# Pacing GpSimd's indirect transfers and thinning TensorE's waits in a graph and mixer network

## The reference, cut to what matters

```python
xn = _layernorm(x, axis=-1)
x = x + _L1_gnn_ref(xn, ...) + _L1_mix_ref(xn[None], ...)[0]
x = x + _L1_ffn_ref(_layernorm(x, axis=-1)[None], ...)[0]
```

```python
h = (x @ W.T).reshape(n, heads, out_ch)
e = jax.nn.leaky_relu(alpha_src[src] + alpha_dst[dst], NEG_SLOPE)
e = jnp.exp(e - m[dst])
alpha = e / (s[dst] + 1e-16)
out = jax.ops.segment_sum(alpha[:, :, None] * h[src], dst, num_segments=n)
```

## Time and profile before

| | |
|---|---|
| median of 3 runs | 10682.89 us (10681.89 to 10693.84) |
| span of the profiled execution | 10685.8 us |
| TensorE busy | 6666.1 us, 62% |
| VectorE busy | 5067.1 us, 47% |
| GpSimd busy | 3649.9 us, 34% |
| ScalarE busy | 2678.2 us, 25% |

### The profile page before, as it was taken

The page is one execution under the profiler, slowest core; times in us unless marked ns, Lnnn a source line. Parts: engine busy times, 40 slices in busy tenths (PEclk is TensorE's granted clock), DMA queues, the critical chain, the costliest instruction groups (busy, mean ns, idle before and its releaser), DMA issues. The chain is left out here.

```text
span 10685.8 us, 95917 instructions
## 1 busy us (share of the span) xinstructions
PE 6666.1 (62%) x27702; PEld 4202.5 (39%) x27702; DVE 5067.1 (47%) x10547; ACT 2678.2 (25%) x6047; POOL 3649.9 (34%) x3597
## 2 busy tenths in 40 slices
PE   5456656689657536649984663665664577626856
PEld 4452333334444433336753332333443233313434
DVE  6453046522477733461126544436545788733231
ACT  0012100022244404302223430331222455312211
POOL 2522346400246436602032763462111355120021
PEclk5558877799779857769996776677787799868968
DMA  3110033210246433304423333331022122210012
GB/s 94 38 34 13 4 89 91 56 46 27 69 136 179 120 98 88 91 6 131 168 83 96 95 90 78 101 91 32 15 67 61 44 68 69 68 58 7 7 60 76
DMA packets 440710, 758.91 MB, mean 71 GB/s; under 512 B 172573, under 2 KB 268795, under 8 KB 437521
## 3 DMA queue, kind: packets, MB, share of 16 engines
q0 software_dynamic: 182080, 437.26, 15.1%
q1 hardware_dynamic: 239987, 295.32, 8.8%
q10 hardware_dynamic: 18136, 20.19, 0.6%
HBM read 669.59 MB, written 82.56 MB: 70 GB/s over the span
## 5 line engine op out<-in xcount | busy, mean ns | idle before, releaser
L2448 POOL DMA_INDIRECT R<-table,edges x1248 | 1243.2, 996 | 861.0 <-issue 306.3
L2500 DVE TENSOR_TENSOR acc<-acc,PS 125x256 f32 (+3 forms) x1664 | 704.9, 424 | 1242.4 <-PE PS L2519 376.5
L2519 PE MATMUL PS<-R,hot 128*125 128x256 f32 (+1 forms) x1664 | 644.8, 476 | 418.0 <-issue 203.4
L2527 PE MATMUL PS<-iota_b,ident_b 128*128 128x500 bf16 x1728 | 764.7, 449 | 5.7 <-PEq L71 5.7
L2268 PE MATMUL PS<-S,hotT 125*128 125x100 bf16 (+1 forms) x6240 | 362.9, 218 | 575.1 <-DVE hotT L2375 460.4
L2460 ACT ACTIVATE R<-R,TW 128x128 f32<-128x128 f32 (+1 forms) x1248 | 493.4, 431 | 685.0 <-DMA R<-table,edges 644.7
L2519 PEld LDWEIGHTS PS<-R,hot 128*125 128x125 f32 x1664 | 361.6, 234 | 683.1 <-issue 520.3
L2517 PE MATMUL PS<-R,hot 128*125 128x258 f32 x1664 | 438.0, 416 | 203.6 <-DVE acc L2498 117.5
L2268 PEld LDWEIGHTS PS<-S,hotT 125*128 125x128 bf16 x6240 | 315.3, 112 | 623.8 <-DVE hotT L2375 429.7
L2448 POOL DMA_INDIRECT xx<-table,edges x416 | 412.8, 992 | 384.4 <-PE PS L2519 312.5
L2448 POOL DMA_INDIRECT room<-table,edges x416 | 425.6, 1023 | 330.2 <-PE PS L2519 191.7
(11 more groups left out here) (719 smaller groups left out, 13558.8 us busy)
## 6 DMA issues: line engine op xcount, KB each, us to landing
rowb<-slo_row SPq DMA_DIRECT2D x260, 250.0 KB
W<-in_L_ffn_W1p SPq DMA_DIRECT2D x32, 1024.0 KB
W<-in_L_ffn_W2p SPq DMA_DIRECT2D x32, 1024.0 KB
near<-dst_row SPq DMA_DIRECT2D x98, 256.0 KB
R<-table,edges POOLq DMA_INDIRECT x1248
W<-in_L_ffn_w SPq DMA_DIRECT2D x16, 1024.0 KB
hib<-hi_mask SPq DMA_DIRECT2D x260, 50.0 KB
g<-gate_rows POOLq DMA_DIRECT2D x8, 1568.0 KB
```

The lines of the kernel that those rows point to most:

```text
L2448: pool.indirect_dma_start(self.R[:, u, 0:self.W], None, self.table[:, :], bass.IndirectOffsetOnAxis(ap=self.G.edges[:, g, 0:1], axis=0)).t ...
L2500: v.tensor_tensor(to, to, self.G.PS[0:P, self.bank + k, 0:self.WH], ALU.add).then_inc(self.put, 1)
L2519: mm = pe.matmul(self.G.PS[0:P, self.bank + k, 0:self.WH], hot, self.R[:, u, :], start=True, stop=True)
L2527: pe.matmul(G.PS[:, 6, 0:4 * P], G.ident_b[:, :], G.iota_b[:, :].unsqueeze(1).to_broadcast([128, 4, P]), start=True, stop=True)
```

## The change

Five edits. The count of landed scatters is split over two semaphores by the parity of the tile, and SP waits for both. In the sort, scatter f waits until scatter f − 2 has landed. In the mixer, each scatter is followed by a memset of a spare buffer of 128x256 on GpSimd and a wait for that memset. In the edge weights, early gather g waits until gather g − 2 has landed. In the edge sums, TensorE's waits per tile are thinned: for the one-hots, tails and low it waits once per four tiles and for one of the three, and for `high` once per two tiles with the count for both.

```diff
--- before.py
+++ after.py
@@ -1752,18 +1752,22 @@
     def __init__(self, G, s, later):
         self.G, self.now = G, FE - later
         self.rows, self.place = s.sb("edge_rows", [128, F, 4], I32), s.sb("edge_place", [128, F], I32)
-        self.scattered, self.fetched = s.sem("scattered"), s.sem("fetched")
+        self.scattered, self.fetched = [s.sem(f"scattered{j}") for j in range(2)], s.sem("fetched")
+        self.rest, self.rested = s.sb("rest", [128, 256]), s.sem("rested")
 
     def send(self, pool, f):
         pool.indirect_dma_start(self.G.sorted[:, :], bass.IndirectOffsetOnAxis(ap=self.place[:, f:f + 1], axis=0),
-                                self.rows[:, f, :], None).then_inc(self.scattered, 16)
+                                self.rows[:, f, :], None).then_inc(self.scattered[f % 2], 16)
 
     def gpsimd(self, pool):
         for f in range(self.now, FE):
             self.send(pool, f)
+            pool.memset(self.rest[:, :], 0.0).then_inc(self.rested, 1)
+            pool.wait_ge(self.rested, f - self.now + 1)
 
     def sync(self, sp):
-        sp.wait_ge(self.scattered, 16 * FE)
+        for j in range(2):
+            sp.wait_ge(self.scattered[j], 16 * len(range(j, FE, 2)))
         sp.dma_start(self.G.edges[:, :, :], self.G.sorted[0:ET * 128, :].rearrange("(p j) w -> p j w", p=128)).then_inc(self.fetched, 16)
         sp.wait_ge(self.fetched, 16)
 
@@ -1868,6 +1872,8 @@
                 for f in range(scatter.now):
                     if f % FB == 0:
                         pool.wait_ge(placed, f // FB + 1)
+                    if f >= 2:
+                        pool.wait_ge(scatter.scattered[f % 2], 16 * (f // 2))
                     scatter.send(pool, f)
 
             @block.tensor
@@ -2223,6 +2229,8 @@
                     pool.dma_start(dT[:, g, :, :], fill[at:at + TT * 128, :].rearrange("(t q) h -> t q h", t=TT)).then_inc(dload, 16)
                 if sums:
                     for g in range(sums.slots):
+                        if g >= 2:
+                            sums.landed(pool, g - 2)
                         sums.gather(pool, g)
 
             @block.sync
@@ -2502,14 +2510,12 @@
     def tensor(self, pe, g):
         u, k, half, b = g % self.slots, g % self.banks, self.WH // 2, g // TB
         hot = self.hot[b % HB][:, g % TB, :]
-        pe.wait_ge(self.hot_done, b + 1)
-        if self.H:
-            pe.wait_ge(self.tails, b + 1)
-            pe.wait_ge(self.high, g + 1)
-        if self.split:
-            pe.wait_ge(self.low, b + 1)
+        if g % TB == 0:
+            pe.wait_ge(self.low if self.split else self.tails if self.H else self.hot_done, b + 1)
         if not self.H:
             self.landed(pe, g)
+        elif g % 2 == 0:
+            pe.wait_ge(self.high, g + 2)
         if g >= self.banks:
             pe.wait_ge(self.put, g - self.banks + 1)
         if self.wide:
```

## The result

The changed kernel takes 10340.43 us in the median of three runs (10318.33 to 10342.57) where the kernel before takes 10682.89: 0.9673 of it, 95% interval 0.9655 to 0.969, or −342 us. It was forecast at 10270.

A forecast was written before the change was run, and what follows sets the result against it. No engine is near full; stages lose time to late TensorE releases while GpSimd issues indirect DMAs back to back. Sort −195, mixer −95, early gathers −125, thinner waits 0 sum to −415 from 10685.8: about 10270, range 10180 to 10490.

The forecast's parts named there:

- the likeliest case: Sort, mixer and early gathers all gain: about 10270 us, own range 10220 to 10380, chance 0.46.
- Releases of what waits for TensorE are late while GpSimd issues indirect DMAs without a pause: Sort, mixer's FFN, edge weights: at 1.26 us between DMAs engines start about 10 to 15 us late; a pause ends it.
- Fill scatters at 1.48 us do no such harm: Edge weights stage: scatters 1.48 us apart leave VectorE no wait on L2268 over 1.6 us.
- Sort −195: Sort with two scatters in flight: 1.5 us per scatter, end at 556 against 751.46; bounds −134 to −220 if working.
- Mixer −95: Mixer's FFN: scatters 1.67 us apart with the memset, GpSimd ends it at 1210 for 1306.36; bounds −110 and −67.
- Early gathers −125: Three edge-weight stages: gathers 1.4 to 2.0 us apart remove waits summing to 132 us; bounds 0 and −132.
- Thinner waits 0: Edge sums: fewer TensorE waits gain 0, since they run beneath the product before and GpSimd paces.
- Rival (e): Sort, mixer, early gathers: any indirect DMA in flight delays TensorE's releases, so throttling costs +172, 10855; chance 0.06.
- Rival (d): Five aggregates: TensorE's fewer waits also unblock GpSimd, −100 to −325 more, 9950 to 10170; chance 0.05.
- GpSimd's rhythm paces them: Edge sums: GpSimd sets the pace, 368 gathers busy 356.4 of 600 us, and the diff doesn't change its rhythm there.
- the rule of the Trainium skill: Sort: a small GpSimd DMA takes about 2.0 us, under 2.26, so the wait never bites and the sort keeps 751.

The follow-up runs named there:

- the ladder: Kernel before, with memset pauses of 256, 128, 64 or 32 columns or none by batch of the sort's scatters, 256 in the mixer; 10561.9 us.
- the kernel with pauses: Changed kernel with a 128x256 memset and a wait for it replacing each landing wait in sort and early gathers; 10333.97 us, ratio 0.9671.
- e7_no_wait: Kernel before plus a 128x256 memset behind each scatter in sort and mixer, no wait between memset and next scatter; 10332.79 us in one run.

## Why the prediction was right, and where it was off

The direction, the places and the reason were right, and the range held the time; the likeliest case came, all three parts working. Two of its three gains were some 40 us too large each; the mixer 8 us better than forecast and 24 us in small steps that it had at nothing took some of that back, and the edge sums' share of these 24 is hardly clear of the scatter between runs. By its steps:

- *Releases of what waits for TensorE are late while GpSimd issues indirect DMAs without a pause.* Shown, on three chips: pauses alone, with nothing else of the change, restore the pace (in the mixer on the first, in the ladder's batch of 256 columns on the second, in sort and mixer on the third). Not a property of every chip: a fourth doesn't have it. The prediction had nothing on that. The trace of the kernel before shows more than the prediction read from it, since it also records when a semaphore rises. In the earlier trace rows ScalarE waits for the products of L1906, which end at 372.54, and VectorE for those of L1910, which end at 372.88, not for L1917. Their semaphores rise at 383.50 and 387.74, and the two engines start at 383.52 and 387.76. So the waiting engines start at once; what comes 11.0 and 14.9 us late is TensorE's increment. And only TensorE's: in the sort (150 to 720 us), of the recorded waits over 1 us that an increment of TensorE ended, 38 of 112 had it over 1 us late, up to 19.0; of those that one of VectorE or ScalarE ended, none of 59. Every timed run here was recorded too, so whether the delay is there without recording no run shows.
- *Fill scatters at 1.48 us do no such harm.* Only next to the others. In their stretch (3805 to 3843 us) 9 of the 11 waits of VectorE on TensorE end with an increment that is 1.0 to 1.7 us late. The first 24 products of L2340 take 39 to 46 us in the five stages of edge weights, and 28 to 30 on the fourth chip, some 67 us in all; that those are the late increments is argued, as it rests on two chips. The change leaves this where it is.
- *Sort −195.* Measured −154 and −150 in the whole change, −145 alone. The wait bites, as read from the 3.46 us of the earlier trace rows. The interval was mis-sized: 1.64 us in the mean and not 1.5, about 1.75 while the loads of near run, 265 × 0.14 = 37 of the 41 us missed. The rest is the 5.3 us from the last scatter to the next stage, for which the sum had no term.
- *Mixer −95.* Measured −103. The interval is 1.57 with rare longer ones, 1.60 in the mean; the 0.1 us for the wait was too much.
- *Early gathers −125.* Measured −88. The waits of 132 us did go (the first stage was 56 us ahead at the 33rd product), but I had put the cost of undelayed gathers at nothing. Beside them the chain is slower, by 14, 4 and 13 us in the three stages from the 33rd product on, and in the kernel with pauses, whose gathers are over early, by 14, 3 and 10. In the first stage the landings of 5 us and more also made the gathers outlast the chain, another 8 us. I had sized the landing from a scatter's, as I had no row for a gather beside these loads.
- *Thinner waits 0.* −10 (−19 to 0) alone. A gain of 2 to 4 us an aggregate may be real.
- *Rival (e), any indirect DMA in flight delays*, is refuted by the pauses: at 1.57 us an interval and landings of over 2.1, some transfer is in flight all the time, and in the sort and the mixer no release is over 1 us late. *Rival (d), the aggregates gain as well*, did not happen, but its ground was sound: on the chip without the delay each of the five aggregates is 70 to 89 us shorter than in the kernel before on its chip, over my estimate of 65 for each (a comparison between chips, thinner waits included). My sentence that GpSimd's rhythm paces them was half the truth.
- By the rule of the Trainium skill ("DMA: Bandwidth & Descriptors", Anatomy of one DMA, SWDGE path) on a GpSimd DMA's 2.0 us the sort would have gained nothing. The trace disagrees beside the loads: the wait bit 70 times, which takes landings of over 2.26 us.

So what limited this change is that GpSimd ended the sort, the mixer and one of the three stages with early gathers, and that gathers slow their stage's chain down. The best version for the chips with the delay is still open: e7_no_wait got some 43 us more from two places than the changed kernel does, in one run, and with early gathers it was never timed there.

## What to carry to other kernels

Look at what an engine off the critical path does in the stretch of a wait that names no local releaser: here a third engine's stream of transfers nearly doubled the time of a batch (50.1 us for 26.4). Where releases come late, a pause of 0.33 us behind each of its transfers gave as much as a wait for a landing, and its price is the longer stream, so work out first which of the two will end the stage. And time such a change on more than one chip.

## What the runs showed of the hardware that was not expected

- Chips differ: the kernel before takes 10627 to 10685 us on three of them and in the result's runs, and 9799 on another, and there no release of TensorE is late beside gathers 1.31 us apart in the mean.
- Where releases are late, waits for them last up to 43.3 us, some 9 of them work. It is TensorE's increments that are late; VectorE's and ScalarE's in the same sort are not, in 59 waits.
- A memset of 128x256 behind each scatter (0.33 us) frees them, with or without a wait for it; one of 128x192 with a wait nearly did (3.9 us a group), one of 128x128 (0.22 us) with a wait did not, in one batch each and on two chips.
- An indirect scatter of 0.96 us took over 1.2 us 40 times in 189 beside a busy VectorE, and 3 times in 50 beside an idle one.
